# An explicit table of places sets the order of 3,921 steps on five queues, in a one-core kernel of two transformer layers

## The reference

```python
# L0 attention: linear attention, then a SiLU FFN 341 wide, each with a layer norm
kv = einsum('bsd,bse->bde', kp, v); attn = (qp @ kv) / (qp . k_sum + eps)
x = layer_norm(x + attn); x = layer_norm(x + (silu(x @ Wg) * (x @ Wu)) @ Wd)
# L0 FFN: 8 experts, all of them on every token, 512 wide, summed
x = sum_e (silu(x @ Wg[e]) * (x @ Wu[e])) @ Wd[e]
# L1 attention: 4 layers of
x = x + project(filter(hamilton(hamilton(quat(q), quat(k)), quat(v))))   # q, k, v from layer_norm(x)
x = x + gelu(layer_norm(x) @ fc) @ mproj
# L1 FFN: each token's best 2 of 8 experts, 512 wide
```

## Time and profile before

| what | value |
|---|---|
| median of 3 runs | 1509.45 us (1508.14 to 1509.75) |
| span of the profiled execution, first to last instruction | 1503.8 us |
| difference between that median and the span | 5.7 us |
| PE busy | 1395.6 us, 93% |
| DVE busy | 1250.3 us, 83% |
| ACT busy | 1042.7 us, 69% |
| POOL busy | 360.9 us, 24% |
| moved by DMA | 238.02 MB, mean 158 GB/s |

### The profile page before, as it was taken

How to read it: one execution, slowest core, us unless ns; L and a number is a source line. 1 busy time by engine, 2 the same in 40 slices (tenths; PEclk the granted TensorE clock), 3 DMA queues, 4 the chain that set the end, 5 groups by cost and what they waited for, 6 DMA issues and landing times.

```text
span 1503.8 us, 20880 instructions
## 1 busy us (share of the span) xinstructions
PE 1395.6 (93%) x6198; PEld 990.6 (66%) x6198; DVE 1250.3 (83%) x1511; ACT 1042.7 (69%) x2411; POOL 360.9 (24%) x251
## 2 busy tenths in 40 slices
PE   6999999999899999899999899999889999999858
PEld 4677766666566666566665667656677677777636
DVE  3344467877999989999959897999999999999996
ACT  6455757676886777766877768777857787776652
POOL 0001203110221402011131411131543353344410
PEclk9999999999999999999999999999999999999989
DMA  7763445335544554533363335355555556555244
GB/s 270 261 255 139 157 146 185 118 114 168 167 135 148 179 164 135 206 117 111 109 216 113 99 107 168 121 155 174 162 184 167 158 176 198 162 174 160 86 112 155
DMA packets 111243, 238.02 MB, mean 158 GB/s; under 512 B 13207, under 2 KB 52844, under 8 KB 109644
## 3 DMA queue, kind: packets, MB, share of 16 engines
q1 hardware_dynamic: 106588, 227.31, 47.9%
q0 software_dynamic: 4544, 9.38, 1.8%
HBM read 185.59 MB, written 43.86 MB: 153 GB/s over the span
## 4 chain that ended last, share of the span: by engine, by line
PE 44%; issue 20%; DVE 16%; ACT 9%; POOL 8%; DMA 2%; SPq 0%; ACTq 0%; POOLq 0%; DVEq 0%
PE bank L1363 8%; PE bank L1351 7%; PE bank L1353 6%; PE bank L1352 6%; POOL RSTD L1025 4%; PE bank L1543 3%; DVE AM L1087 3%; POOL ytok L1040 3%; ACT ROWS L865 2%; PE bank L1458 2%; DVE SH L1217 2%; DVE TA L1083 2%; PE bank L1452 1%; ACT ROWS L878 1%; DVE TA L1092 1%
## 5 line engine op out<-in xcount | busy, mean ns | idle before, releaser
L1025 POOL TENSOR_TENSOR RSTD<-SS,power_half 128x4 f32<-128x4 f32 x96 | 158.8, 1654 | 816.7 <-ACT ROWS L865 816.5
L1363 PE MATMUL bank<-SH,WD 128*128 128x512 f32 x512 | 263.6, 596 | 0.8 <-DVE X L1233 0.8
L1351 PE MATMUL bank<-NH,GU 128*128 128x512 f32 x512 | 245.5, 479 | 2.0 <-DMA GU<-halves 1.0
L1217 DVE TENSOR_TENSOR SH<-SH,bank 128x512 f32<-128x512 f32 x256 | 172.4, 682 | 76.4 <-ACT SH L853 46.4
L1087 DVE TENSOR_TENSOR AM<-AM,TA 128x1024 f32<-128x1024 f32 x192 | 230.2, 1219 | 0.9
L1083 DVE TENSOR_TENSOR TA<-QKV 128x2048 f32<-128x2048 f32 x96 | 219.5, 2287 | 1.2
L1353 PE MATMUL bank<-NL,GU 128*128 128x512 f32 x512 | 203.0, 397 | 0.0
L1352 PE MATMUL bank<-NH,GU 128*128 128x512 f32 x512 | 202.6, 396 | 0.0
L853 ACT ACTIVATE SH<-bank 128x512 f32<-128x512 f32 x256 | 153.1, 605 | 59.6 <-PE bank L1353 57.5
L878 ACT ACTIVATE ROWS<-bank,RSTD 128x128 f32<-128x128 f32 x384 | 110.0, 374 | 56.2 <-POOL RSTD L1025 50.8
L1578 PE MATMUL bank<-XT,GU 128*128 128x256 f32 x624 | 147.5, 381 | 0.3 <-DVE SH L1335 0.3
(11 more groups left out here) (232 smaller groups left out, 2764.8 us busy)
## 6 DMA issues: line engine op xcount, KB each, us to landing
GU<-halves SPq DMA_DIRECT2D x112, 512.0 KB, 4.2
QKV<-QKV SPq DMA_DIRECT2D x32, 720.0 KB
GU<-in_w_gu SPq DMA_DIRECT2D x39, 512.0 KB, 3.6
xg<-in_c_fill SPq DMA_DIRECT2D x8, 2080.0 KB
WD<-in_w_d SPq DMA_DIRECT2D x128, 128.0 KB, 2.2
FC<-ready_w SPq DMA_DIRECT2D x32, 512.0 KB, 5.2
WQ<-ready_w SPq DMA_DIRECT2D x32, 384.0 KB, 4.8
WD<-in_w_d SPq DMA_DIRECT2D x39, 256.0 KB, 3.8
```

The source lines that it names most:

```text
L1025: pool.tensor_tensor(RSTD[:], SS[:], (power_one if k[0] == "at" else power_half)[:], ALU.pow).then_inc(power_done, 1)
L1217: dve.tensor_tensor(SH[:, g % 4, :], SH[:, g % 4, :], banks[2 + g % 2][:], ALU.mult).then_inc(h_ready, 1)
L1351: pe.matmul(out, w_hi, x_hi, start=True, stop=False)
L1363: pe.matmul(banks[4][:], WD1[:, slot, :], SH[:, g % 4, :], start=first, stop=last).then_inc(down_done, 1)
```

## The change

`Plan`, `TUNE` and the simulation in `schedule()` are gone. In their place stands a table `PLACES` with 3,921 numbers: for each name and engine, the place of each key's step in that engine's list. `schedule()` only turns the table into lists, works out the order of the keys, and which half of a buffer each `views` takes. By its description the table comes from a search that models the transfer engines as one queue, in which transfers hold each other up.

```diff
-class Plan:
-    READY = 0.25
...
+PLACES = {
...
+    "fill": {
+        "SP": (35, 36, 66, 88, 101, 143, 174, 207,),
+    },
...
 def schedule():
...
+    every, at = step_keys(), {}
+    for name, engines in PLACES.items():
+        for engine, places in engines.items():
+            mine = [key for key in every[name] if TAKES_PART.get((name, engine), lambda key: True)(key)]
+            for key, place in zip(mine, places):
+                at.setdefault(engine, {})[place] = (name, key)
+    orders = {engine: [steps[i] for i in sorted(steps)] for engine, steps in at.items()}
...
-    sums_before = count_before("ACT", ("keys_exp", "query"), lambda name, key: name == "scale" and key[0] == "at")
+    sums_before = count_before("DVE", ("keys_exp", "query"), lambda name, key: name == "normed" and key[0] == "at")
```

More of the change, by code:

```diff
@@ L161 @@
[L161 to L179, removed]
-}
@@ new lines, with step_keys @@
+TAKES_PART = {
+    ("centre", "DVE"): lambda key: key[0] in ("A", "C"),
+    ("centre", "ACT"): lambda key: key[0] != "at",
+    ("normed", "ACT"): lambda key: key[0] in ("n0", "n1", "n3", "A", "C"),
+    ("normed", "DVE"): lambda key: key[0] != "n3",
+    ("route", "ACT"): lambda key: key[1] in (0, 2),
+    ("route", "PE"): lambda key: key[1] == 2,
+    ("route", "DVE"): lambda key: key[1] != 2,
+}
+def step_keys():
+    lt = [(t, l) for t in range(TILES) for l in range(LAYERS)]
+    scalings = [(kind, t) for kind in ("n0", "at", "n1", "n2", "n3") for t in range(TILES)]
+    scalings += [(kind, t, l) for kind in ("A", "C") for t, l in lt]
+    tiles, blocks = list(range(TILES)), list(range(BLOCKS))
+    twice = [(g, i) for g in blocks for i in range(2)]
+    out = {name: list(range(n)) for name, n in (
+        ("raw", EXPERTS), ("split", EXPERTS), ("keep", EXPERTS), ("visit", TILES * SPAN // 2), ("split_attn", 1),
+        ("load_prep", LAYERS), ("prep", LAYERS), ("prep_centre", LAYERS), ("keep_prep", LAYERS), ("load_gain", 1),
+        ("last_down", 1), ("kv_sum", BATCHES), ("load_numbers", 1), ("table", 2))}
+    for name in ("fill", "add_experts", "keys", "keys_exp", "query", "ffn2_down", "ffn2_add", "save", "logits", "load_kept",
+                 "total", "load_y", "back", "merge", "out"):
+        out[name] = tiles
+    for name in ("load_w", "load_x", "turn_in", "down", "y_out"):
+        out[name] = blocks
+    for name in ("gate_up", "silu", "mult", "y_store"):
+        out[name] = twice
+    for name in ("load_q", "load_f", "load_p", "load_m", "roll", "turns", "differences", "reduce", "cosines", "fold", "freq",
+                 "gain", "proj", "proj_add", "fc_a", "fc_b", "mproj", "mlp_add", "round"):
+        out[name] = lt
+    for name in ("centre", "power", "scale", "turn", "normed"):
+        out[name] = scalings
+    out["den"] = [(t,) for t in tiles]
+    out["expert"] = [(t, s) for t in tiles for s in range(SPAN)]
+    out["ffn2"] = [(t, c) for t in tiles for c in range(3)]
+    out["route"] = [(t, i) for t in tiles for i in range(4)]
+    out["scatter"] = [(t, i) for t in tiles for i in range(2 * GROUPS)]
+    out["views"] = [(t, l, j) for t, l in lt for j in range(VIEWS)]
+    out["ham"] = [(t, l, i) for t, l in lt for i in range(HAM + 2)]
+    return out
```

533 lines of the change are left out of this document (350 added, 183 removed), and 129 rows, old and new, of the table PLACES.

## The result

The changed kernel takes 1483.41 us (median of 4 runs, 1482.21 to 1485.05) beside 1508.9 (4 runs, 1508.14 to 1509.75): a ratio of 0.9832, interval 0.9818 to 0.9846, or 25.5 us less. The forecast was 10.4 us less; the time lies in the forecast's range, near its lower end, but the gain is 2.5 times the one forecast. It is, within 2 us, what rival D said (1485), to which I had given 0.20. Two single runs of later comparisons, one of before with 7089 us and one of experiment 11's kernel with 3619 us, lie far outside all others and count in no ratio.

A forecast was written before the change was run, and what follows sets the result against it. PE was taken as the bound up to 1400 us, then a chain from norm to norm. Eight gap terms summed to -20.7 us; half, -10.4, was taken from 1509.45, giving 1499.0 us, range 1482 to 1514.

The forecast's parts named there:

- rival D: Whole sum arrives, with part of d and gaps too short to list: -24, 1485 us; chance 0.20.
- a: At 32.71 us, prep(0) waits for keys behind a weight split on DVE; keys now goes first: -3.0 us.
- b: At mproj(3, 0), PE waits 2.3 us for the MP load behind the seventh fill; fill moved behind it: -2.3 us.
- c: Around 787.55 us, DVE waits for a roll issued behind a fill, PE for the QKV copy; both links cut: -5.0 us.
- d: At 849.65 us, a turn waits 3.28 us for ACT; an expert moves between centre and turn: 0 us.
- e: At 1070.53 us, a centre waits 3.32 us for a DVE norm behind a route; turn and centre now earlier: -2.0 us.
- f: At 1297.72 us, a turn waits 2.77 us; down products now ahead of it, their mult ahead of a ham: -2.5 us.
- g: At 1413.44 us, fc_a(7, 2) waits 2.63 us; products now fill the gap: -2.5 us.
- h: At the end, mproj(7, 2) ahead of a freq, differences ahead of a normed, down products filling a gap: -3.4 us.
- The marks to look for: MP waits within 1 us, DVE's 3.83 us gap gone, turn waits under 30, clock at least 0.985, same PE busy time.
- B: Gaps only move: chains set PE's idle time, so closing eight gaps opens eight others; 1509 us, chance 0.12.
- C: Slower: experts placed ahead of turns make turns late by 2.24 us each; +7.5, 1517 us, chance 0.18.

The follow-up runs named there:

- experiment 11: Same run as e8: kernel before with only keys(0) moved ahead of split(2) on DVE; 1506.52 us, ratio 0.9989.
- e6: Kernel before with the change's order only at the seven places a, b, c, e, f, g, h; 1507.13 us, ratio 0.9989.
- e8: Kernel before with one step moved, keys(0) ahead of split(2) on DVE; 1506.52 us, ratio 0.9989.
- e17: The places of e6 on PE, DVE and ACT, plus the change's whole SP and POOL lists, else as before; 1504.03 us, ratio 0.9972.
- e1: Kernel before with SP's whole list of the change, the other four lists as before; 1515.46 us, ratio 1.0049 to before.
- e5: Kernel before with only the eight fills on SP at the change's places; 1501.72 us, ratio 0.9957 to before.
- e12: The change with ready work moved into three of its remaining PE gaps; 1489.07 us, ratio 0.9862 to before.
- e11: The change with seven turns on PE put back ahead of the expert that preceded them; 1486.01 us, ratio 0.9860 to before.
- e7: The change with the order of before at places b, c, e, f, g, h, keeping a; 1512.93 us, ratio 1.0032 to before.
- e9: Kernel before up to 1100 us, all five lists of the change from there on; 1503.13 us, ratio 0.9957 to before.
- e16: The whole change with POOL's list as before, other four lists as changed; 1490.30 us, ratio 0.9893 to before.
- e2: The change with the eight fills put back behind the SP steps they followed before; 1499.74 us, ratio 0.9946 to before.
- e10: As e9 (the change's lists from 1100 us on), but with POOL's list as before; 1510.23 us, ratio 1.0013 to before.

## Why the prediction was wrong

The direction, the reason (gaps of PE and the clock behind them) and the range were right; the size was wrong, by one step and what it stood on: the halving of the sum, with nothing put in for the moves that had no term.

**The halving.** "I don't expect all of it to arrive ... I take half." From the table of shifts, the listed places gave -4.8 (a), -0.4 (b), -5.8 (c), +0.8 (d), -0.9 (e), -2.3 (f), -1.9 (g) and +0.8 (h), together -14.5 where half of the sum was -10.4. And the places that I had not listed, which the sum put at nothing, gave the other -8.9 of the 23.4. So what failed is the halving together with the zero for all other moves. I had two reasons for the half. The first, that the terms were read in the old timing, is true of an edit in otherwise old lists, and stronger than I put it (e6: 0 to -4 us of -20.7 by its interval; e8 decides nothing). It isn't true of lists in which the steps behind are placed for the new timing. The 316 and 666 moves, which I read as a risk, were the part that made the terms arrive (e17: the places with SP's and POOL's new lists give -4, with the other moves on PE, DVE and ACT -25.5). The second reason, DVE at 96% from 1100 to 1400 us, left 12 us of idle time there; the change used 5.8 of them.

**By its terms.** a, c and f were right in size, and a and c include fills. b was right in its place (-2.5 there, as in e1, e5 and e6), with 2.1 given back by 649 us. But its price was read from one execution, in which it was low: the wait was 2.31 us in the trace of before and 2.66 to 4.60 in five other executions with the old lists there, in four of them with the product behind it slowed to 5.4 us from 3.70. The profiled execution of before was some 3 us under its median (1505.6 beside 1508.9), and that of the change 1.2 us under its own, which is why the medians differ by 25.5 us and the spans by 23.4. d, at zero, was right: the gap is still 2.22 us long at 836.21. g came at three quarters. e (-2.0 forecast, -0.9 found) and h (-3.4 forecast, +0.8 found) didn't come. At h the down products did go ahead of the turn, but the gap before the turn is 4.73 us long still, at 1425.21, and the one before, 5.52 at 1411.48, was 4.28. The chain of norms and DVE set the end there, as I had written myself, so a PE step moved into a gap gave nothing.

**The marks to look for.** The wait for MP and DVE's gap are gone, the clock is over 0.985; but PE's waits for turns, which I wanted under 30 us, are 41.6, and the "same busy time of PE" was wrong, as I had counted the clock in the terms and forgotten it in the mark.

**The rivals.** B (gaps only move) is what the single moves of e12 do. C has nothing for it: e11. D came within 2 us, and had 0.20 since I took DVE's busy share as a wall. Its sentence "the order fits as one whole" is what e6, e7, e9 and e16 show. Its number is in part luck: the listed places gave -14.5 and not -20.7, d did not close, and the unlisted places made up for both. What stays open is how the gain divides among PE's, DVE's and ACT's lists.

The rule of "DMA: Bandwidth & Descriptors" in the Trainium skill (section "Why a DMA increments its semaphore by 16 and not by 1") on how many engines a transfer runs, which spoke against b, found no case: the fill's harm did not go to the visit behind it, as PE's products never wait for GU in the trace of the change. The trace does agree with it only in that a load behind a fill lands late (14.39 us in e2, 12.81 in the earlier trace rows, against a median of 4.8); no run shows on how many engines the fill ran.

## What to carry to other kernels

Price a new order as a whole: the gain of a stretch in which all queues change together, less the waits that remain, not a sum of gaps cut by half for safety. Conversely, an order read gap by gap can't be mended gap by gap; a single move should be made where nothing waits for the moved step (a fill), and measured to the end of the kernel, since what it wins can be lost at a late load (e2) or at the end (e6). And read a gap in more than one execution before it becomes a term. A queue that is 24% busy, like POOL's here, can still hold everything up by the order of what it waits for.

## What was not expected of the hardware

A lasting shift is nearly exact: PE's steps in experiment 2's kernel, whose compute lists are those of the change, are 14.0 to 14.1 us behind the change's all the way from 860 to 1070 us. But at a few places executions of the same lists part by 1 to 4 us: at the load of MP by 0.3 to 4.0, and at 1000 us by 1.2 (e9) and 2.8 (e10). And more than half of the gain (13.0 of 23.4 us) was clock, not idle time: thirteen stretches at or near the lower level of 1.2 of 2.4 GHz in the trace of before, nearly all of them right behind an idle time of PE of over a microsecond, became six. Whether the lists of the change also run more evenly isn't shown: its 4 runs reach over 2.8 us, the 4 of before beside them over 1.6, while 71 runs of before in all reach from 1503.3 to 1512.4.
